# Expert rows that carry a gate and are added to the output by an indirect DMA, residuals stored during attention

## What is computed

```python
x = L0_attn_x                                    # (16, 256, 128)
mod = (_silu(L0_c) @ L0_wmod).reshape(16, 6, 1, -1)
sa, ca, ga, sb, cb, gb = (mod[:, 0], ..., mod[:, 5])    # ga, gb pushed to |.| >= 0.25
h = _layernorm(x) * (1 + ca) + sa
x = x + ga * attn(h, W_Q, W_K, W_V, W_O)
h = _layernorm(x) * (1 + cb) + sb
x = x + gb * ffn(h, ...)

def ffn(x, ...):
    xn = x * rsqrt(mean(x * x) + eps) * ln_w
    vals, idx = top_k(xn @ Wg + bg, 2); topk_w = softmax(vals)
    # for each token: sum over its two experts e of
    #   topk_w * ((silu(xn @ W1a[e] + b1a[e]) * (xn @ W1b[e] + b1b[e])) @ W2[e] + b2[e])
```

## Time and profile before

| | |
|---|---|
| three runs | median 564.38 us (563.98 to 567.52) |
| profiled execution | 564.96 us |
| its span, first to last instruction | 563.1 us |
| busy in the span | PE 451.6, DVE 438.5, ACT 369.4, POOL 325.0 us |

### The profile page before, as it was taken

One profiled execution on the slowest core, in us unless ns is written; L12 is line 12 of the kernel. 1 busy time (PEld: TensorE's weight loads), 2 busy tenths in 40 slices (PEclk: granted clock), 3 DMA queues, 4 the chain that ended last, 5 costly groups with the idle time before them and its releaser, 6 DMA issues.

```text
span 563.1 us, 20014 instructions
## 1 busy us (share of the span) xinstructions
PE 451.6 (80%) x6425; PEld 327.0 (58%) x6426; DVE 438.5 (78%) x1378; ACT 369.4 (66%) x916; POOL 325.0 (58%) x469
## 2 busy tenths in 40 slices
PE   4689999998988988889889313999999999999300
PEld 2445556665555655555555212988888888888300
DVE  4478888999999999999984661777777777777366
ACT  2347777877768777776864221988889888898300
POOL 3433355677777777877766772145455554545553
PEclk9999999999899999998995555999999999999855
DMA  7311111122102222022111323122222112121086
GB/s 216 122 30 46 33 34 39 55 69 63 61 16 69 69 64 59 18 67 70 36 42 40 99 77 102 31 59 66 53 57 59 48 53 57 50 57 36 15 266 181
DMA packets 46920, 37.74 MB, mean 67 GB/s; under 512 B 9234, under 2 KB 41573, under 8 KB 46848
## 3 DMA queue, kind: packets, MB, share of 16 engines
q1 hardware_dynamic: 36288, 25.05, 16.3%
q0 software_dynamic: 4544, 8.54, 4.7%
q10 hardware_dynamic: 6016, 3.21, 1.9%
HBM read 24.77 MB, written 12.78 MB: 67 GB/s over the span
## 4 chain that ended last, share of the span: by engine, by line
PE 35%; DVE 34%; issue 10%; ACT 8%; DMA 4%; SPq 4%; POOL 2%; DVEq 1%; ACTq 1%; POOLq 0%
DVE nmax L799 8%; PE bank L1315 4%; PE bank L1316 4%; PE bank L1317 4%; PE bank L1127 3%; DVE xhat L767 3%; PE bank L1336 3%; DVE probs L1029 3%; ACT qk_t L670 2%; PE bank L1169 2%; PE bank L1337 2%; PE bank L1134 2%; DVE hl L1016 2%; PE bank L1147 2%; PE bank L1338 2%
## 5 line engine op out<-in xcount | busy, mean ns | idle before, releaser
L563 POOL DMA_INDIRECT expert_outs<-probs,number_of x78 | 78.6, 1007 | 95.1 <-ACT probs L699 80.3
L799 DVE TENSOR_REDUCE nmax<-bank 128x2 f16<-128x384 f32 (+1 forms) x192 | 114.8, 600 | 20.6 <-PE bank L1134 18.5
L611 ACT ACTIVATE probs<-bank 128x512 f32<-128x512 f32 (+1 forms) x192 | 100.6, 524 | 45.6 <-PE bank L1159 44.6
L1029 DVE SCALAR_TENSOR_TENSOR probs<-bank,b_sb,probs 128x256 f32<-128x256 f32 x156 | 71.7, 479 | 53.0 <-ACT probs L710 52.3
L1127 PE MATMUL bank<-qk_t 24*64 24x64 f16 (+3 forms) x1024 | 74.5, 246 | 28.5 <-DVE nmax L799 19.4
L1315 PE MATMUL bank<-xt,we_hi 128*128 128x256 f16 x312 | 86.2, 276 | 2.8 <-DVE probs L1029 1.2
L1316 PE MATMUL bank<-xt,we_hi 128*128 128x256 f16 x312 | 86.0, 276 | 0.0
L1317 PE MATMUL bank<-xt,we_lo 128*128 128x256 f16 x312 | 85.9, 275 | 0.0
L480 POOL DMA_INDIRECT expert_rows<-send,pos_i x64 | 64.7, 1010 | 26.0 <-DVE tok L884 14.3
L690 ACT ACTIVATE hh<-probs 128x256 f16<-128x256 f32 x156 | 64.2, 411 | 20.3 <-DVE probs L1029 18.2
L1147 PE MATMUL bank<-qk_t 32*64 32x256 f16 (+3 forms) x1024 | 72.5, 240 | 1.7 <-DMA qk_t<-nmax_t 1.6
(11 more groups left out here) (157 smaller groups left out, 1087.3 us busy)
## 6 DMA issues: line engine op xcount, KB each, us to landing
g_in<-expert_rows SPq DMA_DIRECT2D x39, 132.0 KB
qk_t<-nmax_t SPq DMA_DIRECT2D x256, 0.5 KB
mod_b<-mod_rows SPq DMA_DIRECT2D x16, 256.0 KB
we_lo<-expert_outs SPq DMA_DIRECT2D x16, 256.0 KB, 3.8
wstage<-in_L_ffn_W1a_dram SPq DMA_DIRECT2D x16, 128.0 KB
wstage<-in_L_ffn_W1b_dram SPq DMA_DIRECT2D x16, 128.0 KB
wstage<-in_L_ffn_W_dram SPq DMA_DIRECT2D x16, 128.0 KB
out_dram<-we_lo ACTq DMA_DIRECT2D x16, 128.0 KB, 3.4
```

The costliest lines, as they stand in the source:

```text
L563: pool.indirect_dma_start(out=outs, out_offset=bass.IndirectOffsetOnAxis(ap=number_of[:, r, s:s + 1], axis=0), in_=y_sb[:, r, s, :], in_of ...
L611: nc.scalar.activation(probs[:, k // 3, first:end], col_bank[k % 2][:, 0:end - first], ACT.Exp, scale=SM_SCALE).then_inc(probs_ready, 1)
L799: nc.vector.tensor_reduce(nmax[:, pair, js[0]:js[-1] + 1, 3 * DK + c], scores, AX.X, ALU.max, negate=True).then_inc(max_ready, 1)
L1029: nc.vector.scalar_tensor_tensor(out=h32[:, f], in0=banks[f][:, TS:2 * TS], scalar=b1_sb[:, 1, bass.ds(e * FB + f, 1)], in1=silu_a[:, f], ...
```

## The change

The rows in `expert_rows` grow from 132 to 260 words; the last 128 hold the gate row of the token's batch. SyncE loads this row into all rows of the `send` buffer, once a batch (`gates`), and the first send of the batch waits for it (`gate_in`). VectorE in place of ScalarE does the weighing, and multiplies weight and gate at once; it stands behind the first of the tile's four steps and needs the loaded rows until then, so that the load that reuses them waits for it (`vec_w`). Token numbers count tokens, not slots. The residual `x_sb` of a batch is stored to the output during attention, by SyncE, and the scatter of the expert tiles adds to the output (`compute_op=ALU.add`). Two tiles can hold the same token, so the scatter of tile j waits for the landing of tile j-1. The last pass, `expert_outs` and the load of all gates are gone.

```diff
-ROWW = D + 4
-W_IDX, W_WGT = D, D + 1
-NOUT = B * S * K
+ROWW = 2 * D + 4
+W_IDX, W_WGT, W_GATE = D, D + 1, D + 4
+NOUT = B * S
...
@@ sync, iteration
                 if s1:
                     place_max(i + 1, 1)
+                if routing:
+                    sp.wait_ge(pool3a.sem, pool3a.after(i - 2, "resid"))
+                    sp.dma_start(out_view[:, NS * (i - 2):NS * (i - 1), :], x_sb[:, NS * (i - 2):NS * (i - 1), :]).then_inc(x_out, 16)
+                if placing:
+                    gates(i - 3)
+
+            def gates(b):
+                if due(b // 2):
+                    sp.wait_ge(sent[b % 2], 64 * (b // 2))
+                sp.dma_start(send[:, b % 2].rearrange("p k s w -> p (k s) w")[:, :, W_GATE:], mod_rows[b:b + 1, 3 * D:].unsqueeze(1).broadcast_to([P, K * NS, D])).then_inc(gate_in[b % 2], 16)
...
-            sp.wait_ge(probs_used, B * 2 * HG)
-            sp.dma_start(gb_sb, mod_rows[:, 3 * D:].unsqueeze(0).broadcast_to([P, B, D])).then_inc(gb_in, 16)
...
@@ sync, load of a tile's rows
                     sp.wait_ge(named.sem, named.after(plus(j, -4), "weight"))
                     sp.nop(nofuse=True)
+                    sp.wait_ge(vec_w, times(plus(j, -4), NS, NS))
+                    sp.nop(nofuse=True)
...
@@ gpsimd
             def send_rows(b, n):
                 s, k = n // K, n % K
+                if n == 0:
+                    pool.wait_ge(gate_in[b % 2], 16 * (b // 2 + 1))
                 pool.wait_ge(vec_place.sem, vec_place.after(b, "pos_i"))
...
@@ gpsimd, scatter
-                pool.wait_ge(act_y, times(j, NS, NS))
+                pool.wait_ge(vec_w, times(j, NS, NS))
+                before = plus(j, -1)
+                if due(times(before, 1, 1)):
+                    pool.wait_ge(y_sent[before[1]], times((before[0], 0, 1), 32, 32))
                 pool.nop(nofuse=True)
                 for s in range(NS):
-                    pool.indirect_dma_start(out=outs, out_offset=bass.IndirectOffsetOnAxis(ap=number_of[:, r, s:s + 1], axis=0),
-                                            in_=y_sb[:, r, s, :], in_offset=None, bounds_check=NOUT - 1, oob_is_err=False).then_inc(y_sent[r], 16)
+                    pool.indirect_dma_start(out=out_rows, out_offset=bass.IndirectOffsetOnAxis(ap=number_of[:, r, s:s + 1], axis=0),
+                                            in_=y_sb[:, r, s, :], in_offset=None, bounds_check=NOUT - 1, oob_is_err=False, compute_op=ALU.add).then_inc(y_sent[r], 16)
...
@@ scalar: weigh and the stores of the last pass are gone
-                    nc.scalar.activation(y_sb[:, r, s], yb[:, r % 2, s], ACT.Copy, scale=weight_of[:, r, s:s + 1]).then_inc(act_y, 1)
...
@@ vector, tile
                     nc.vector.scalar_tensor_tensor(out=h32[:, f], in0=banks[f][:, TS:2 * TS], scalar=b1_sb[:, 1, bass.ds(e * FB + f, 1)],
                                                    in1=silu_a[:, f], op0=ALU.add, op1=ALU.mult).then_inc(vec_h, 1)
+                    if f == 0 and finished:
+                        weigh(plus(j, -2))
...
+            def weigh(j):
+                r = j[1]
+                vec.wait_ge(vec_y, times(j, 1, 1))
+                vec.wait_ge(named.sem, named.after(j, "weight"))
+                if due(times((j[0], 0, 1), 32)):
+                    vec.wait_ge(y_sent[r], times((j[0], 0, 1), 32))
+                vec.nop(nofuse=True)
+                for s in range(NS):
+                    nc.vector.scalar_tensor_tensor(out=y_sb[:, r, s], in0=yb[:, r % 2, s], scalar=weight_of[:, r, s:s + 1],
+                                                   in1=g_in[:, r, s, W_GATE:], op0=ALU.mult, op1=ALU.mult).then_inc(vec_w, 1)
...
@@ vector, last pass
-                nc.vector.tensor_tensor(ygate[:, r], ysum[:, r], gb_sb[:, bass.ds(times(n, 1), 1), :].broadcast_to([P, NS, D]), ALU.mult).then_inc(vec_gate, 1)
...
-                nc.vector.tensor_tensor(res[:, r], ygate[:, r], x_sb[:, bass.ds(times(n, NS), NS), :], ALU.add).then_inc(vec_res, 1)
```

More of the change, by code:

```diff
@@ L219, in build @@
         y_sb = early[:, 2 * FB * TS:2 * FB * TS + 4 * NS * D].rearrange("p (r s d) -> p r s d", s=NS, d=D)
[L222 to L231, removed]
         banks = [ctx.enter_context(nc.psum_tensor(f"bank{i}", [P, 512], F32)) for i in range(8)]
@@ L289, in build @@
         pe_ab, act_silu, vec_h, act_hh, vec_hl = sem("pe_ab"), sem("act_silu"), sem("vec_h"), sem("act_hh"), sem("vec_hl")
-        pe_y, vec_y, act_y = sem("pe_y"), sem("vec_y"), sem("act_y")
+        pe_y, vec_y, vec_w = sem("pe_y"), sem("vec_y"), sem("vec_w")
         y_sent = [sem(f"y_sent{r}") for r in range(4)]
-        y_back = [sem(f"y_back{r}") for r in range(4)]
-        pool_sum, vec_gate, vec_res = sem("pool_sum"), sem("vec_gate"), sem("vec_res")
-        out_done = [sem(f"out_done{r}") for r in range(4)]
         TABLE_STEPS = 18
@@ L356, in build @@
         x_view = x_in.rearrange("b (s p) d -> p (b s) d", p=P)
+        out_view = out.rearrange("b (s p) d -> p (b s) d", p=P)
         w1a_v = w1a.rearrange("e d (h f) -> e h d f", h=NS)
@@ L448, in _ @@
                 sp.wait_ge(y_sent[r], 32 * ((NT - r + 3) // 4))
[L449 to L459, removed]
         @block.gpsimd
@@ L570, in _ @@
             scatter(tile_number(NT - 1), False)
-            def finish(n):
-                m, r, _ = n
-                pool.wait_ge(y_back[r], times((m, 0, 1), 16, 16))
-                if due(times(plus(n, -4), 1, 1)):
-                    pool.wait_ge(vec_gate, times(plus(n, -4), 1, 1))
-                nc.gpsimd.tensor_tensor(ysum[:, r], y_in[:, r, :, 0, :], y_in[:, r, :, 1, :], ALU.add).then_inc(pool_sum, 1)
-            in_fours(pool, 0, B, finish)
         @block.scalar
@@ L690, in high, with tile @@
                 nc.scalar.activation(hh[:, j[1] % 2, f], h32[:, f], ACT.Copy).then_inc(act_hh, 1)
-            def weigh(j):
-                r = j[1]
-                if due(times((j[0], 0, 1), 32)):
-                    act.wait_ge(y_sent[r], times((j[0], 0, 1), 32))
-                act.wait_ge(vec_y, times(j, 1, 1))
-                act.wait_ge(named.sem, named.after(j, "weight"))
-                for s in range(NS):
-                    nc.scalar.activation(y_sb[:, r, s], yb[:, r % 2, s], ACT.Copy, scale=weight_of[:, r, s:s + 1]).then_inc(act_y, 1)
             known_experts, read_next_experts = experts_of(act)
-            def tile(j, more=True, finished=True):
+            def tile(j, more=True):
                 e = known_experts(j)[0]
@@ L712, in tile @@
                         save_x(plus(j, 1))
-                    if f == 2 and finished:
-                        weigh(plus(j, -2))
                     if f == 2:
@@ L721, in _ @@
             save_x(tile_number(0))
-            tile(tile_number(0), finished=False)
-            tile(tile_number(1), finished=False)
-            in_fours(act, 2, NT - 1, tile)
+            in_fours(act, 0, NT - 1, tile)
             tile(tile_number(NT - 1), more=False)
-            weigh(tile_number(NT - 2))
-            weigh(tile_number(NT - 1))
-            out_v = out.rearrange("b (s p) d -> b p s d", p=P)
-            def store(n):
-                m, r, _ = n
-                act.wait_ge(vec_res, times(n, 1, 1))
-                act.dma_start(out_v[times(n, 1)], res[:, r]).then_inc(out_done[r], 16)
-            in_fours(act, 0, B, store)
         @block.vector
@@ L1041, in bias_out @@
                 if due(times(plus(j, -2), NS, NS)):
-                    vec.wait_ge(act_y, times(plus(j, -2), NS, NS))
+                    vec.wait_ge(vec_w, times(plus(j, -2), NS, NS))
                 y = (o_bank, tail_bank)[j[1] % 2]
@@ L1365, in constants @@
         for s in range(NS):
-            c[:, C_TOK + k * NS + s] = K * (s * P + p) + k
+            c[:, C_TOK + k * NS + s] = s * P + p
     c[:, C_POW:C_POW + 4] = -0.5
```

18 lines of the change are left out of this document (7 added, 11 removed).

## The result

| | before | after |
|---|---|---|
| median of four runs each, side by side | 564.92 us | 720.62 us (719.89 to 723.71) |
| ratio | | 1.2757, 95% interval 1.2700 to 1.2815 |
| profiled execution / its span | 564.96 / 563.1 us | 720.87 / 719.0 us |

The account below looks back on a forecast made before the run. VectorE was taken to bound attention, TensorE the expert stage. From 564.96 us, -28.0 (last pass), +24.9 (serial scatters) and +22 (gate wait) gave 583.9, or 583.3 against the runs' median; range 554 to 606 us.

Parts of the forecast that it names:

- last pass gone: End of kernel: the 28.37 us behind the last scatter's landing go, 0.4 us kept for the program's end; -28.0 us.
- up to the last `xhat` of attention: Attention: GpSimd's first send waits for the late gate load, delaying rstd and stopping VectorE; about +22 us.
- from there to the first scatter: Seam before the experts: wider rows cost about 0.8 us, the first weighing comes about 0.8 us earlier.
- first scatter to last landing: Expert stage: scatters become a serial chain of 5.1 us a turn, 198.1 us in place of 173.27; +24.9 us.
- The landing of the gate load: Attention: the load of 256 KB in 512 B pieces lands after 3.3 us, between 2.2 and 4.5.
- The chain: Expert stage: each scatter waits for the previous tile's landing; 5.1 us a turn, above the tile's 4.54, so GpSimd sets the pace.
- Wrong in kind if TensorE waits for loaded rows: Expert stage: the sign that would show the forecast mistaken in kind, not only in size; no size given.
- Edits put at nothing: Weighing on VectorE, loads waiting for the weighing, wider rows at the seam and residual stores: together no net cost.
- The load loop: Expert stage: a tile's load waits for the weighing four tiles before; 8.7 us for two tiles, under 9.08, so covered.
- Nearly free: Expert stage: adding scatters land within 2.46 us, tiles stay at 4.54 us; 559 to 560 us, chance 0.18.
- The gate is in time: Attention: the gate lands within about 1.3 us of issue and VectorE never stops; 563 us, chance 0.12.
- The addition is slow: Expert stage: a scatter turn over 5.7 us, landing over 3.6; 607 us and more, chance 0.08.

Follow-up runs that it names:

- the early load: Changed kernel with SyncE issuing each batch's gate load first in its list for the iteration, not last; 608.83 us.

## Why the prediction was wrong

The sum, with what each step measured in the changed kernel. From 564.96 to 720.87 us are 155.9 us:

| step | forecast | measured | from |
|---|---|---|---|
| last pass gone | -28.0 | -24.8 | 28.4 go, but 3.6 us lie behind the last landing (715.40 to 719.0), 0.4 were kept |
| up to the last `xhat` of attention | +22 | +114.5 | 436.47 - 321.97 |
| from there to the first scatter | 0 (+0.8 - 0.8) | +6.6 | 46.1 - 39.5 |
| first scatter to last landing | +24.9 | +59.6 | (715.40 - 482.53) - 173.27 |
| sum | +18.9 | +155.9 | |

(198.1 less 173.27 is 24.8; the 24.9 of the sum is a slip of 0.1.)

- **The landing of the gate load is the step that failed.** I put it at 3.3 us, between a load of 256 distinct rows and a line through two broadcasts. Its bounds rested on bytes. The 1024 KB row reads 16 rows 128 times each; this load reads one row 512 times, and no row shown did that. It took 8.5, outside both bounds. From a landing of 3.5 us to one of 8.5 the last `xhat` moves from 374.8 to 436.5 us, 12.3 us for each us of landing; 5.2 us too little are 64 of the 92 us missed here.
- **The rest of that term**: only VectorE's direct stop was priced. At a landing of 3.5 us that stop was right to 0.4 us (2.4 an iteration for 2.0). But ten iterations, put at +18, took 41.2 us more: waiting for TensorE in turn (10.3 us) and VectorE's longer instructions (7.8 us) stood in no term. With the last iterations (7.7 us for 4.0) this is some 27 us.
- **The chain: right in its mechanism, one of its terms mis-sized.** The forecast turn was 0.8 + 1.28 + 3.0 = 5.1; it is 0.8 + 1.86 + 3.3 = 6.0, and (6.01 - 5.1) x 38 = 34.6 us are the 34.7 missing. I let only the landing grow (+0.7, measured +1.0) and left the instruction at its plain length, while I argued that it must describe a second read. GpSimd does set the pace, as said, and TensorE's last matmul starts at 692.2 us, with four tiles of scatters left (two or three were forecast). But VectorE did not wait for the four buffers of the weighed tile. It waits for `weight_of`, since the names of tile j+2 stand behind the scatter of tile j-1 in GpSimd's list. The stall came sooner; the end is the same.
- **"Wrong in kind if TensorE waits for loaded rows":** it does, 61.5 us (22.5 of them for the first tile's), but this wait follows the chain: with the loads freed from the weighing it falls to 46.5 us and tiles stay 6.0 us apart.
- **Edits put at nothing: three were not.** The load loop was given 8.7 us for two tiles and called just covered; under the chain it is, without the chain it costs 20.3 us (556.77 to 536.43). The weighing on VectorE is covered, as said (348 ns each, forecast 344), but moving it off ScalarE is worth 14 us: "TensorE sets the pace" was read from a busy share of 98%, and it was not its floor. At the seam SyncE's pads land after 8.5 us (3.8 before) and the last batch's first send waits 4.0 us for its gate; no run takes the 6.6 us apart.
- **The rivals.** "Nearly free" needed a landing up to 2.5 us. It was 3.3. By the fit of the Trainium skill (DMA: Bandwidth & Descriptors, section Anatomy of one DMA — SWDGE (gpsimd) path), with twice the bytes, the adding landing would have been an estimated 2.3 us: the trace does not agree for the adding scatter (3.3), and does for the plain one (an estimated 2.15, measured 2.3). "The gate is in time" is what the early load makes true, with 608.83 us in place of the 563 of that rival, for the turn of 6.0 and the seam. "The addition is slow" began at a turn of 5.7 and put 607 us there: it is what came in the expert stage, with 0.08 of my chance.

## What to carry to other kernels

A load's landing is bounded by rows that read memory in the same way: count how often the same row is read, not only bytes and pieces. When a new wait falls on the engine that sets the pace, price also what the others lose behind it, and first see whether the transfer can be issued an iteration earlier. A busy share of 98% does not make an engine the bound; look at what the engine that feeds it waits for.

## What the runs showed of the hardware

- One 512 B row of memory read 512 times by one DMA lands after 8.5 us, read 256 times after 4.9; 512 different rows after 3.5. About 14 ns for each further read of the same row.
- An indirect DMA that adds, 128 rows of 512 B: its instruction 1.56 us for 0.98, landing 3.3 us for 2.3, and 128 packets of 512 B for 16 of 4,096 B.
- TensorE busy 78.26 of 80 us did 914 matmuls, busy 80.00 it did 996, at a granted clock of 1.00 both times; its weight loads were busy 67.80 and 74.77 us.
